# Column halves, values for four pairs at once, and another order in a two-layer attention kernel

## The reference

```python
xn = layernorm(x)
x = x + attn0(xn) + ffn0(xn)
xn = layernorm(x)
x = x + attn1(xn) + ffn1(xn)
```

## Time and profile before

| | |
|---|---|
| median of 3 runs | 2595.58 us (2592.46 to 2601.22) |
| the profiled execution | 2594.35 us, of it 2592.6 us from the first to the last instruction |
| busy PE, ACT, DVE, POOL | 94%, 73%, 72%, 55% of the span |
| mean granted TensorE clock | 0.987 of full speed |
| matmul records | 18176 |

### The profile page before, as it was taken

One profiled execution on the slowest core, in us unless ns is written; L12 is line 12 of the kernel. 1 busy time (PEld: TensorE's weight loads), 2 busy tenths in 40 slices (PEclk: granted clock), 3 DMA queues, 4 the chain that ended last, 5 costly groups with the idle time before them and its releaser, 6 DMA issues.

```text
span 2592.6 us, 52477 instructions
## 1 busy us (share of the span) xinstructions
PE 2434.2 (94%) x18176; PEld 1228.9 (47%) x18176; DVE 1854.1 (72%) x5637; ACT 1886.2 (73%) x4707; POOL 1416.4 (55%) x1356
## 2 busy tenths in 40 slices
PE   6999999999999999999999999999999999999877
PEld 3554444454544445444554545445454454544431
DVE  4448677677777777677776877777777776867675
ACT  4767787777778777787777778777787778777445
POOL 4866474655646466474655646465474654646311
PEclk8999999999999999999999999999999999999988
DMA  3002020110202002020100202001020200202020
GB/s 92 6 5 50 6 54 2 36 24 6 54 6 50 6 15 45 6 54 2 44 17 6 54 6 50 6 18 42 6 54 2 50 10 6 54 2 54 2 54 5
DMA packets 59829, 68.55 MB, mean 26 GB/s; under 512 B 11056, under 2 KB 55344, under 8 KB 56368
## 3 DMA queue, kind: packets, MB, share of 16 engines
q1 hardware_dynamic: 59568, 65.21, 11.2%
HBM read 35.04 MB, written 29.36 MB: 25 GB/s over the span
## 4 chain that ended last, share of the span: by engine, by line
PE 79%; DVE 9%; ACT 7%; issue 3%; DMA 1%; POOL 0%; SPq 0%; POOLq 0%; DVEq 0%; ACTq 0%
PE pj L1432 21%; PE sc L1494 11%; PE pj L1524 11%; PE op L1551 8%; PE sc L1511 6%; PE sc L1595 5%; PE pj L1450 5%; PE sc L1581 5%; PE pj L1538 5%; DVE pq L1195 3%; DVE mx L1248 2%; PE pj L1424 2%; ACT pt L987 2%; ACT pt L965 1%; ACT pq L947 1%
## 5 line engine op out<-in xcount | busy, mean ns | idle before, releaser
L816 POOL TENSOR_SCALAR pq<-pq,rsum 128x128 f32<-128x128 f32 (+3 forms) x1024 | 1113.0, 1101 | 962.6 <-DVE rsum L1202 962.4
L1248 DVE TENSOR_REDUCE mx<-sc 128x1 f32<-128x512 f32 x1024 | 654.5, 683 | 207.4 <-PE sc L1595 206.5
L987 ACT ACTIVATE pt<-sc 128x512 f32<-128x512 f32 x1024 | 556.5, 608 | 199.9 <-PE sc L1581 198.0
L1195 DVE CUSTOM_DVE_ANT_0 pq<-sc,relkey 128x128 f32<-128x128 f32 (+3 forms) x1024 | 451.0, 488 | 222.1 <-PE sc L1494 215.9
L947 ACT ACTIVATE pq<-pq,mx 128x128 f32<-128x128 f32 (+3 forms) x1024 | 571.4, 573 | 7.1 <-DVE mx L1195 7.1
L965 ACT ACTIVATE pt<-sc 128x512 f32<-128x512 f32 (+1 forms) x768 | 356.9, 533 | 226.9 <-PE sc L1511 224.9
L1494 PE MATMUL sc<-K,Q 64*128 64x128 f32 (+3 forms) x2048 | 378.1, 466 | 18.2 <-DVE mx L1248 10.3
L1524 PE MATMUL pj<-pt,v 128*64 128x512 f32 (+3 forms) x2048 | 308.3, 443 | 9.9 <-DVE y L1216 4.0
L1432 PE MATMUL pj<-xnT,wqkv 128*128 128x512 f32 x512 | 283.4, 645 | 11.6 <-ACT xnT L895 5.5
L1511 PEld LDWEIGHTS sc<-ident,pq 64*128 64x128 f32 x5120 | 203.1, 139 | 164.4 <-issue 121.2
L1511 PE MATMUL sc<-ident,pq 64*128 64x64 f32 x5120 | 235.8, 227 | 26.3 <-DVE mx L1195 22.3
(11 more groups left out here) (117 smaller groups left out, 2878.1 us busy)
## 6 DMA issues: line engine op xcount, KB each, us to landing
scr_p<-y SPq DMA_DIRECT2D x160, 128.0 KB, 2.4
QS<-scr_p SPq DMA_DIRECT2D x30, 384.0 KB, 6.1
KS<-scr_p SPq DMA_DIRECT2D x30, 384.0 KB, 8.8
x_in<-in_L_attn_x SPq DMA_DIRECT2D x16, 256.0 KB, 2.8
scr_p<-tanh SPq DMA_DIRECT2D x32, 128.0 KB, 2.4
out_x<-xres SPq DMA_DIRECT2D x15, 256.0 KB, 2.3
QS<-nrow SPq DMA_DIRECT2D x180, 4.0 KB
wqkv<-in_L_attn_w_qkv SPq DMA_DIRECT2D x1, 1536.0 KB, 6.8
```

The lines of the kernel that those rows point to most:

```text
L816: pool.tensor_scalar(rows, rows, rsum[:, p % NROWS, c:c + 1], None, ALU.mult).then_inc(s_scl, 1)
L987: act.activation(pt1[:, GS * (m % 2) + 2 * j + h, :], sc[tile_bank(i, "st1", 2 * n + h)][:, :], ACT.Exp, scale=float(DS) ** -0.25).then_in ...
L1195: dve.tensor_tensor_reduce(out=pq[:, at:at + width], in0=sc[tile_bank(i, "mx0", m)][:, left:left + width], in1=relkey[:, T - width:T], sca ...
L1248: dve.reduce_max(mx1[:, g % 2, at:at + 1], sc[tile_bank(i, "mx1", 2 * t + h)][:, :], AXIS.X).then_inc(s_mxd1, 1)
```

## The change

It has four parts.

1. `project`, `ffn_second` and `attention_out` issue each product with 128 weight columns as two with 64, on the two column halves. The moving operand of the two is the same. Transposes stay whole.
2. `project_v` is no longer called for each pair with four 128x128 products. It is called eight times for an element; each call takes one block of 128 tokens and the values of four pairs, one product with 512 moving columns. The buffer `v0` holds eight pairs in place of four.
3. `project_q` and `project_k` stand next to each other at the end of `r == 3`, two pairs ahead (lag -2), in place of two places in `r == 0`, one pair ahead. `copy_q` now comes first in ACT's `r == 0`; `copy_k` stays where it was.
4. The order of the calls on PE, ACT, DVE and POOL changes, with many of the constants; `pj_order` and `score_order` follow PE's new order. The layernorm scratch (`stats`, `mv`, `veps`, `rstd`) gets its own copy for each layer. The branches for pair calls in ticks with `late(g)`, in which no pair is left, go.

On ACT `exp0(0)` and `exp0(1)` move into `r == 1`, `exp0(2)` to the end of `r == 2`. On DVE `row_max0(2)` and `row_max0(3)` stay in `r == 2` and `r == 3`; `others` moves to the front of `r == 1` and `r == 2`.

```diff
 TICKS = 4 * NPAIR
-X_AT = -19
-LN0_AT = (-15, -8, -1)
-XNT0_AT = -5
-HT0_AT = -1
-FFN0_AT = (1, 2, 6, 7)
+X_AT = -18
+LN0_AT = (-15, -8, -2)
+XNT0_AT = -6
+HT0_AT = 0
+FFN0_AT = (1, 1, 6, 7)
 FA_AT = 11
-WOA_AT = 35
-WOB_AT = 45
-LN1_AT = (47, 48, 54)
+WOA_AT = 34
+WOB_AT = 44
+LN1_AT = (48, 49, 54)
 XNT1_AT = 49
 ROPE_AT = (51, 52)
-STORE_AT = (49, 50)
-STACK_AT = (54, 54)
+STORE_AT = (50, 50)
+STACK_AT = (59, 63)
 VALS_AT = 54
 HT1_AT = 55
 L1_AT = 58
 L1_TICKS = 28
 FFN1_AT = (56, 56, 59, 60)
-FB_AT = 62
+FB_AT = 63
 TAIL_AT = 86
 TURN3_AT = 87
 OT_AT = 90
 OUT_AT = 91
-HID0_AT = (2, 5, 7, 10)
-HID1_AT = (57, 59, 60, 61)
-ADDA_AT = 11
-ADDB_AT = 64
+HID0_AT = (2, 6, 8, 9)
+HID1_AT = (58, 59, 60, 61)
+ADDA_AT = 12
+ADDB_AT = 63
 ADDWA_AT = 35
-ADDWB_AT = 45
-TURN_ROPE_AT = (52, 53)
+ADDWB_AT = 46
+TURN_ROPE_AT = (52, 54)
 HEAD3A_AT = 87
 HEAD3B_AT = 89
 ADDOUT_AT = 91
-PLN0_AT = (-9, -7)
-PLN1_AT = (47, 48)
-RES0_AT = 0
-RES1_AT = 53
+PLN0_AT = (-11, -7)
+PLN1_AT = (48, 50)
+RES0_AT = 5
+RES1_AT = 52
 HEAD3P_AT = 87
-STOREOUT_AT = 91
+STOREOUT_AT = 95
...
-        v0 = sb("v0", [P, NBUF, NT, P])
+        v0 = sb("v0", [P, NPAIR, NT, P])
...
                     small(g, h, k)
                 elif r == 1:
+                    p, i = pair(g, 1)
+                    if i is not None:
+                        scale_probs(i, p, 3)
                     small(g, h, k)
+                    p, i = pair(g, 0)
+                    if i is not None:
+                        scale_probs(i, p, 0)
                 elif r == 2:
...
 
-            def values(i, p):
-
-                before, was = (i, p - NBUF) if p >= NBUF else (i.ago(1), p - NBUF + NPAIR)
-                if before.live():
-
-                    b, u = pj_use(before, f"pv{was}")
+            def values(i, n):
+
+                half, k = divmod(n, NT)
+                if k == 0 and i.ago(1).live():
+
+                    b, u = pj_use(i.ago(1), f"pv{HP * half + HP - 1}")
                     act.wait_ge(s_pjf[b], u)
-                b, u = pj_use(i, f"v{p}")
+                b, u = pj_use(i, f"v{n}")
                 act.wait_ge(s_pjf[b], u)
-                act.activation(v0[:, p % NBUF, :, :], pj[b][:, :].rearrange("p (t d) -> p t d", t=NT), ACT.Copy).then_inc(s_pje[b], 1)
+                act.activation(v0[:, HP * half:HP * (half + 1), k, :], pj[b][:, :].rearrange("p (c d) -> p c d", c=HP),
+                               ACT.Copy).then_inc(s_pje[b], 1)
...
                     c = T // pieces
-                    last = pe.matmul(t[:, c * k:c * (k + 1)], w(k), x(k), start=True, stop=True)
+                    for j in range(2):
+                        r = slice(DH * j, DH * (j + 1))
+                        last = pe.matmul(t[r, c * k:c * (k + 1)], w(k)[:, r], x(k), start=True, stop=True)
                 last.then_inc(full, 1)
 
             def ffn_first(i, l, f):
...
                 for k in range(NT):
                     for f in range(NF):
-                        last = pe.matmul(t[:, D * k:D * (k + 1)], y[:, f, P * k:P * (k + 1)], w2[:, l, D * f:D * (f + 1)],
-                                         start=f == 0, stop=f == NF - 1)
+                        for j in range(2):
+                            at = P * k + DH * j
+                            last = pe.matmul(t[DH * j:DH * (j + 1), D * k:D * (k + 1)], y[:, f, at:at + DH], w2[:, l, D * f:D * (f + 1)],
+                                             start=f == 0, stop=f == NF - 1)
                 last.then_inc(full, 1)
...
 
-            def project_v(i, p):
-
-                project(i, f"v{p}", lambda k: xnT[:, P * k:P * (k + 1)], lambda k: wqkv[:, 2 * INNER + P * p:2 * INNER + P * (p + 1)], NT)
+            def project_v(i, n):
+
+                half, k = divmod(n, NT)
+                if n == 0:
+                    b, u = pj_use(i, "xnT0")
+                    pe.wait_ge(s_pje[b], u)
+                at = 2 * INNER + HP * P * half
+                project(i, f"v{n}", lambda _: xnT[:, P * k:P * (k + 1)], lambda _: wqkv[:, at:at + HP * P], 1)
 
...
                 pe.wait_ge(s_ev, i.upto(N_TURN, 6 * p + 6))
-                b, u = pj_use(i, f"v{p}")
-                pe.wait_ge(s_pje[b], u)
+                if p % HP == 0:
+                    for n in (NT - 2, NT - 1):
+                        b, u = pj_use(i, f"v{NT * (p // HP) + n}")
+                        pe.wait_ge(s_pje[b], u)
                 t, full = bank(i, f"pv{p}")
...
                     for k in range(NT):
-                        last = pe.matmul(t[:, D * k:D * (k + 1)], att[:, ATT_SLOT[p], P * k:P * (k + 1)], wout[:, p, :],
-                                         start=c == 0 and k == 0, stop=c == HP - 1, skip_group_check=True)
+                        for j in range(2):
+                            at = P * k + DH * j
+                            last = pe.matmul(t[DH * j:DH * (j + 1), D * k:D * (k + 1)], att[:, ATT_SLOT[p], at:at + DH], wout[:, p, :],
+                                             start=c == 0 and k == 0, stop=c == HP - 1, skip_group_check=True)
                 last.then_inc(full, 1)
...
                     transpose4(i, "hT0", lambda k: hn[:, k, :])
+                for n in range(2 * NT):
+                    if (i := at(g, V0_AT[n])) is not None:
+                        project_v(i, n)
...
@@ -1727,15 +1703,9 @@
                     others(g, h, k)
                     second_turns(h, k, 1)
                 elif r == 0:
-                    p, i = pair(g, -1)
-                    if i is not None:
-                        project_q(i, p)
                     second_keys(h, k, 0)
                     second_tops(h, k, 0)
                     second_turns(h, k, 0)
-                    p, i = pair(g, -1)
-                    if i is not None:
-                        project_k(i, p)
                     p, i = pair(g, 0)
                     if i is not None:
                         max_scores0(i, p, 0)
@@ -1743,59 +1713,60 @@
                     if i is not None:
                         turn_probs(i, p, 1)
                     second_values(h, k, 0)
-                    second_values(h, k, 1)
                     others(g, h, k)
                     p, i = pair(g, 2)
                     if i is not None:
                         turn_probs(i, p, 2)
                     second_turns(h, k, 1)
+                    second_tops(h, k, 1)
                     second_keys(h, k, 1)
-                    second_tops(h, k, 1)
+                    second_values(h, k, 1)
                 elif r == 1:
                     second_turns(h, k, 0)
-                    p, i = pair(g, 3)
-                    if i is not None:
-                        pv0(i, p)
                     second_keys(h, k, 0)
                     second_tops(h, k, 0)
+                    second_turns(h, k, 1)
+                    p, i = pair(g, 3)
+                    if i is not None:
+                        pv0(i, p)
+                    second_keys(h, k, 1)
+                    others(g, h, k)
                     second_values(h, k, 0)
+                    second_values(h, k, 1)
+                    second_tops(h, k, 1)
+                elif r == 2:
+                    second_turns(h, k, 0)
+                    p, i = pair(g, 0)
+                    if i is not None:
+                        max_scores0(i, p, 2)
+                    second_keys(h, k, 0)
+                    second_tops(h, k, 0)
                     others(g, h, k)
                     second_keys(h, k, 1)
                     second_tops(h, k, 1)
+                    p, i = pair(g, 0)
+                    if i is not None:
+                        max_scores0(i, p, 3)
+                    second_values(h, k, 0)
                     second_turns(h, k, 1)
-                    p, i = pair(g, 0)
-                    if i is not None:
-                        max_scores0(i, p, 2)
-                    second_values(h, k, 1)
-                elif r == 2:
-                    second_turns(h, k, 0)
-                    second_keys(h, k, 0)
-                    second_tops(h, k, 0)
-                    p, i = pair(g, -1)
-                    if i is not None:
-                        project_v(i, p)
-                    second_keys(h, k, 1)
-                    second_tops(h, k, 1)
-                    second_values(h, k, 0)
-                    others(g, h, k)
-                    second_turns(h, k, 1)
-                    p, i = pair(g, 0)
-                    if i is not None:
-                        max_scores0(i, p, 3)
                     second_values(h, k, 1)
                 else:
                     second_turns(h, k, 0)
-                    second_turns(h, k, 1)
+                    second_values(h, k, 0)
                     second_keys(h, k, 0)
                     second_tops(h, k, 0)
-                    second_values(h, k, 0)
                     others(g, h, k)
                     p, i = pair(g, 1)
                     if i is not None:
```

(19 more changed lines are left out.)

112 lines of the change are left out of this document (41 added, 71 removed).

## The result

The changed kernel takes **2618.59 us** (median of 4 runs, 2615.32 to 2621.82) against 2594.59 (2592.46 to 2601.22) before: ratio **1.0088 [1.0065, 1.0111]**. It is slower by 24 us, where 2526 and "faster" were forecast. The profiled execution has a span of 2620.0 us and a mean granted clock of 0.976.

What follows compares the result with a forecast made beforehand. It took PE to bound the kernel, busy 2434.2 of 2592.6 us. Tiling changes 31.0, uncovered loads 35.4 and passes 8 made 74 us less, 5 given back for ACT: 2526 us, range 2482 to 2576 (chance 0.76).

Steps and rivals of the forecast that it cites:

- What PE bounds: PE sets the time: busy 2434.2 of 2592.6 us and 79% of the chain that ended last.
- Changes of tiling and uncovered loads: On PE, 320 fewer changes of tiling at 0.097 us save 31.0 us; fewer uncovered first weight loads save 35.4 us.
- Passes of 128 columns, the instruction queue, common data: PE's shorter rounds, fewer seams and bf16 loads save 8 us; more instructions and shared moving data cost nothing.
- rivals 3 and 4: Instruction queue can't feed rounds of four, 2680, chance 0.04; halves reading the same data don't overlap, about 3260, chance 0.02.
- DVE, ACT, POOL.: Their instructions stay the same, load about 79% and 77% on DVE and ACT; only ACT's full stretch costs, 0.3 us an element.
- the sum: 74 us off PE, 5 us given back for ACT's full stretch: median 2526, an element about 150.4 us.
- POOL gets scalings earlier in its list; it waited for DVE anyway: POOL's moved work was taken to cost nothing; no size was given.
- Merging q and k: On PE, q and k side by side give 16 of the 23 fewer changes of tiling an element, at 0.097 us each.
- Rival 1: The new order makes PE wait 2 to 4 us more an element: 2574 (2552 to 2588), chance 0.21.
- waits beyond 5 us: A slower outcome from PE's waits growing by over 5 us an element, chance 0.04.
- SP, stacks: SP's queue keeps its order; the keys' stack stays hidden with a margin of about 3 us.

Runs made afterwards that it cites:

- e11: The kernel before with parts 1 and 2 (column halves, values for four pairs) and no change of order: 2568.76 us, 0.9886.
- e1: The changed kernel with one constant back, `RES1_AT` 52 to 53 (POOL's `residual1` at its old tick): 2581.68 us, 0.9948 to the kernel before.
- e7: e1 with a second constant back, `WOA_AT` 34 to 35 (the first `attention_out` at its old tick): 2566.62 us, 0.9893.
- e10: e7 with q and k apart again, in their old places in `r == 0`: 2559.87 us, 0.9848.
- e2: The kernel before with part 1 alone (column halves in `project`, `ffn_second` and `attention_out`), order untouched: 2565.86 us, 0.9886.
- e5: The kernel before with q moved beside k in `r == 0`, one pair ahead as before, nothing else: 2655.77 us, 1.0226.
- e8: e2 with the edit of e5 on top (column halves, q beside k in `r == 0`): 2626.23 us, 1.0119.
- e14: The changed kernel with q and k apart as before, nothing else: 2611.69 us, 1.0058.
- e12: e5 with `row_max1` reading 128 of its 512 columns and the exponent of layer 1 scaled down, so other output: 2605.53 us, 1.0031.
- e13: The kernel before with `row_max1` reading 128 of its 512 columns and the exponent of layer 1 scaled down, so other output: 2559.71 us, 0.9858.

## Why the prediction was wrong

The balance by experiments, in us: parts 1 and 2 in the old order −26 (e11), and from there to the changed kernel +50 (2618.6 − 2568.8), which is what the new order with q and k side by side costs. The place of `residual1` is 37 of it (after to e1) and that of the first `attention_out` 15 (e1 to e7); without the two, e7 stands 2 us under e11, within the intervals. So two constants that moved by one tick hold the whole loss against the kernel before. They don't hold the whole error of the forecast: with both back, e7 stands 41 us above 2526. The rest of the order nets to nothing, a filling that is 18 us shorter against elements that take 1 us more each (e7 and e11); adjacent q and k, which cost 7 us (e10), were expected to give 20.

- **What PE bounds**: right. PE stayed the engine with the longest chain.
- **Changes of tiling and uncovered loads**: the loads are right in price. e2 tests them and the halves' rounds: 28.6 against 28. The price of a change of tiling, 31 of the 74 us, no run tests alone. It fits where it can be seen: q and k together take 1.87 us, forecast 1.8, and e10, with 196 changes more, has PE busy for 25 us more, where 25 were expected.
- **Passes of 128 columns, the instruction queue, common data** (rivals 3 and 4): rounds of two matmuls and two loads run at the forecast pace: `attention_out` with its 32 rounds takes 3.64 us (1188.09 to 1191.73), 0.11 a round with its entry. The rule of the Trainium skill that was weighed in the prediction ("TensorE: Matmul & The Clock Gate", section "Wait — 56ns, not 53.3ns?"), 62 ns for each of the 64 matmuls, would make it 3.97; the trace disagrees, and e2 doesn't show the 35 us. The page gives the figure for hardware decode off, and no run here shows whether it was on.
- ***DVE, ACT, POOL.* — the step that failed.** It ended in "that covers the new order unless a stretch is full" and gave back 0.3 us an element for one full stretch of ACT. If the 4.6 us of work that the sum takes off an element are right, the 157.6 us that an element took in place of 154.9 mean that waits and the slower clock grew by 7.3 us an element, where 0.3 was set. The clock is 1.5 of it (12 stretches of 1.65 us in 13 elements), which no term of the sum had, and the wait of `pv0` another 1.6. I also read the distances between PE's records again with the prices of the prediction (columns, 0.1 us for a change of tiling, the first load of a call of 512 columns) and took what is left as waits. This is an estimate: another way to count the first loads moves each figure by 10 to 35 us and leaves their order. Over the 2000 us from 300 to 2300 it gives 151 us before, 158 in e11, 190 in e7, 217 in e5 and 225 in the changed kernel, the clock's part included. That is 11.7 us an element before (12.9 elements) and 17.7 after (12.7 elements). Many of these waits are under 0.1 us and lie within the modelled end of a record, so the page counts them as busy, and products at 1.2 GHz are busy for longer; that is why PE's busy time fell by only 14 us.
- **"POOL gets scalings earlier in its list; it waited for DVE anyway"**: this priced POOL's moved work by what POOL waits for. What it cost is what DVE, and behind it PE, waits for: 37 us from two additions of 1.27 us once an element. That `RES1_AT` moved stood in the diff and was not priced.
- **Merging q and k**: the sum counted 16 changes of tiling an element less, and the trace of e5 has some 13 less (1490 in 2000 us against 1717). But in the old order the merge costs 60 us (e5, e8) instead of giving 20. The likely reason is that the pair of calls had a second use: each is 1 us in which PE needs no score bank while ACT and DVE empty the five, and side by side they leave longer runs of score calls. In the new order it costs 7 (e14, e10). The waits of e5 speak for spacers, but this isn't shown: e10 gained far less than that theory expected, and by e12 and e13 `row_max1`'s reading is at most a quarter of it.
- **Rival 1** had the direction: the order makes PE wait. Its places were wrong: it named the two `pj` banks taken by q and k and the second projection of tick 1. The waits came at the score banks, and at a `pj` bank in another place, where `pv0` needs the one that a rotary product still holds. Its price of 2 to 4 us an element was too small, and waits beyond 5 us had a chance of 0.04.
- **SP, stacks**: right, no new wait of weight on a transfer.

## What to carry to other kernels

A price for each uncovered first load and each change of tiling, read out of a timeline, forecast a change that touches only PE's own work: 28.6 us measured for 28, nearly all of it loads. But an order is not free because the engines' mean load is under 80%: for each call that moves, look at what the *other* engines run at its new place (a two-input POOL addition beside two-input DVE work first of all), and at how long PE then goes without feeding them, or without letting them empty the banks. Merging two calls that need none of the contended banks can cost more in waits than it saves in work: here 60 us in one order and 7 in another. And set the filling, the steady part and the end of a pipeline beside each other before saying that two orders are worth the same.

## What was not expected of the hardware

- DVE's additions and products of two 128x128 SBUF operands take 0.29 us, and 1.22 to 1.31 us when they begin beside a 128x512 POOL addition of 1.27 us: they end 0.15 us after it. In the middle of POOL's scalings the same instruction took 0.27 us.
- The granted clock fell to 0.50 for about 3.4 us behind a stretch that PE spent two thirds busy (3.35 of 5.00 us) with one wait of 1.57 us in it, and behind one with 3.53 of 4.37 us busy and several short waits. Each cost an element 1.65 us. The wait of 1.57 us stood in 13 steady elements, and such a stretch followed it in 7.
- PE issued rounds of two 128-column half products with their two loads at 0.11 us, for 32 rounds on end, with the same moving data in the two halves.
